# Two hardware loops over octets written out as straight code with constant semaphore counts

## What is computed

```python
x = x + tanh(g_xattn[0]) * L0_xattn(ctx, layernorm(x), mask)   # 2 heads of 64, rms-normed q and k
x = x + tanh(g_ffn[0])   * L0_ffn(layernorm(x))                # 16 experts x 64 slots, soft dispatch/combine
x = x + tanh(g_xattn[1]) * L1_xattn(ctx, layernorm(x))         # 8 heads of 128
x = x + tanh(g_ffn[1])   * L1_ffn(layernorm(x))                # 8 experts, top 2 of them by a router

# L0_ffn: logits = x . slots; dispatch = softmax over tokens; combine = softmax over slots
#   slots = dispatch^T x; eout = (gelu(slots Wg + bg) * (slots Wu + bu)) Wd + bd; out = combine eout
# L1_ffn: y_e = (silu(x Wg_e) * (x Wu_e)) Wd_e; out = sum_e share_e * y_e, share 0 but for the top 2
```

## Time and profile before

| | us |
|---|---|
| median of three executions | 1766.96 |
| the profiled execution | 1768.4 |
| its span (first to last instruction) | 1766.6 |
| TensorE busy with matmuls | 1585.7 (90%) |
| TensorE weight loads | 1320.4 (75%) |
| VectorE busy | 1113.1 (63%) |
| ScalarE busy | 965.1 (55%) |
| GpSimd busy | 396.7 (22%) |

### The profile page before, as it was taken

How to read it: one execution, slowest core, us unless ns; L and a number is a source line. 1 busy time by engine, 2 the same in 40 slices (tenths; PEclk the granted TensorE clock), 3 DMA queues, 4 the chain that set the end, 5 groups by cost and what they waited for, 6 DMA issues and landing times. The chain is left out here.

```text
span 1766.6 us, 35984 instructions
## 1 busy us (share of the span) xinstructions
PE 1585.7 (90%) x12837; PEld 1320.4 (75%) x12837; DVE 1113.1 (63%) x2407; ACT 965.1 (55%) x1470; POOL 396.7 (22%) x346
## 2 busy tenths in 40 slices
PE   1677479999999999999999998699989979999998
PEld 1566368888887888878888886577777747888887
DVE  6688476666666666666666654366666656555555
ACT  1678366676676666666666664366556543222222
POOL 2243332222322223222232221122223200000000
PEclk9899799999999999999999999799999989999999
DMA  8100000000000000000000000200000020000000
GB/s 224 34 1 0 16 1 2 1 2 1 2 2 3 1 1 2 2 3 1 2 2 1 2 1 25 74 1 1 0 0 0 1 73 1 7 12 6 6 6 12
DMA packets 31166, 23.43 MB, mean 13 GB/s; under 512 B 3161, under 2 KB 28721, under 8 KB 30898
## 3 DMA queue, kind: packets, MB, share of 16 engines
q1 hardware_dynamic: 31026, 21.56, 4.4%
HBM read 19.46 MB, written 2.10 MB: 12 GB/s over the span
## 5 line engine op out<-in xcount | busy, mean ns | idle before, releaser
L887 ACT ACTIVATE gelu<-psG,b_cols 128x512 f32<-128x512 f32 x256 | 176.1, 688 | 178.2 <-PE psG L137 164.4
L987 PE MATMUL psDown<-w_down,hidden 128*64 128x128 f32 x4096 | 252.0, 276 | 0.6 <-DVE expert_out L774 0.6
L768 DVE SCALAR_TENSOR_TENSOR hidden<-psU,b_cols,gelu 128x512 f32<-128x512 f32 x256 | 189.5, 747 | 88.5 <-ACT gelu L887 66.1
L987 PEld LDWEIGHTS psDown<-w_down,hidden 128*64 128x64 f32 x4096 | 220.9, 137 | 18.4 <-DVE expert_out L774 9.0
L1632 ACT ACTIVATE silu<-psG 128x512 f32<-128x512 f32 x128 | 76.4, 597 | 213.2 <-PE psG L137 207.6
L774 DVE TENSOR_TENSOR expert_out<-psDown,b_down 128x512 f32<-128x512 f32 x128 | 88.2, 689 | 157.5 <-PE psDown L987 147.2
L723 POOL TENSOR_TENSOR combine_sum<-combine_sum,combineT 128x512 f32<-128x512 f32 x48 | 61.2, 1276 | 350.9 <-ACT combineT L901 350.9
L1694 PEld LDWEIGHTS psY<-w_downT,hidden 128*128 128x128 f32 x1024 | 124.0, 191 | 5.8
L1694 PE MATMUL psY<-w_downT,hidden 128*128 128x128 f32 x1024 | 124.3, 275 | 0.0
L1586 DVE TENSOR_TENSOR hidden<-psU,silu 128x512 f32<-128x512 f32 x128 | 88.5, 692 | 54.6 <-PE psU L137 51.3
L1575 DVE SCALAR_TENSOR_TENSOR x<-psY,combine,x 128x128 f32 (+1 forms) x256 | 72.7, 345 | 78.1 <-PE psY L1694 77.8
(11 more groups left out here) (326 smaller groups left out, 3627.1 us busy)
## 6 DMA issues: line engine op xcount, KB each, us to landing
ctx<-in_ctx SPq DMA_DIRECT2D x8, 512.0 KB, 7.2
x<-in_x SPq DMA_DIRECT2D x4, 512.0 KB, 5.5
w_gate_raw<-in_L_ffn_Wg SPq DMA_DIRECT2D x1, 2048.0 KB, 12.8
w_up_raw<-in_L_ffn_Wu SPq DMA_DIRECT2D x1, 2048.0 KB, 18.3
out<-x SPq DMA_DIRECT2D x8, 256.0 KB, 2.3
w_kv<-in_L_xattn_Wkv SPq DMA_DIRECT2D x1, 1024.0 KB
w_down_raw<-in_L_ffn_w_down SPq DMA_DIRECT2D x1, 1024.0 KB, 10.4
kv<-in_L_ffn_slot_embeds SPq DMA_DIRECT2D x1, 512.0 KB, 4.2
```

Source lines behind the costliest of these rows:

```text
L768: dve.scalar_tensor_tensor(hid[e][:, half, :], U[half][:], bcol[:, 1, 4 * ch + 2 * e + half:][:, 0:1], gel[half][:], ALU.add, ALU.mult).th ...
L887: act.activation(gel[half][:], G[half][:], ACT.Gelu, bias=bcol[:, 0, 4 * ch + 2 * e + half:][:, 0:1]).then_inc(s["gelu"], 1)
L987: last = pe.matmul(DN[e * SEQ:(e + 1) * SEQ, j, :], hid[e][:, half, b * SEQ:(b + 1) * SEQ], wd[:, 2 * ch + e, half, :], start=(half == 0 a ...
```

## The change

Both hardware loops become Python loops, so that every octet is emitted once with constant counts and addresses. No instruction of the computation is added, removed or reordered; each engine's order of octets, chunks and slots stays.

```diff
@@ walk
     body(-1, 1)
     body(0, 0)
-    if OCTETS > 2:
-        with eng.Fori(0, (OCTETS - 2) // 2) as turn:
-            body(turn * 2 + 1, 1)
-            body(turn * 2 + 2, 0)
+    for o in range(1, OCTETS - 1):
+        body(o, o % 2)
     body(OCTETS - 1, 1)
@@ stage_experts1
         def octets(eng, body):
-            body(0)
-            with eng.Fori(1, OCTETS) as o:
+            for o in range(OCTETS):
                 body(o)
```

## The result

The changed kernel takes 1752.91 us (median of 4 executions, 1752.04 to 1754.48), the kernel before 1766.26 beside it (4 executions, 1765.21 to 1768.95): a ratio of 0.9923, 95% interval 0.9906 to 0.994. The forecast was 1753.9.

A forecast was written before the change was run, and what follows sets the result against it. It took TensorE to bound both experts stages, short waits through VectorE and ScalarE besides TensorE in attention 1, and VectorE to be mostly busy in attention 0. 8.6 + 4.0 + 0.3 + 0.2 = 13.1 off 1766.96 gave 1753.9 us, range 1750 to 1762.

The forecast's parts named there:

- The jumps, 6.1: Experts 0, two far jumps back: 4.78 us of TensorE idle time and 1.36 after it go; 6.1 us, bounds 4.8 and 6.1.
- The octet edges, 1.2: Experts 0, edges into octets 1 to 6: first gate product starts 0.20 us sooner after its copy; 1.2 us in all.
- Chunks 4 and 6, 1.0: Experts 0, looped octets: these chunks drop from 13.13 to the straight 13.05 us; 1.0 us over six octets.
- `finish`, 0.3: Experts 0, VectorE's register instructions elsewhere in an octet: 0.3 us, between 0 and 0.6, from 0.1 for each octet.
- Attention 1, 4.0: Six looped octets: transposes stop waiting for hats, 1.58 us, and earlier hats shorten a later idle time, 2.4; bounds 1.0 and 4.4.
- the second gain: Attention 1: hats beginning sooner shorten TensorE's 1.12 us idle before the output product to 0.7; 0.40 x 6 = 2.4 us.
- The rest: Attention 0 gains 0.3 us (bounds -0.5 and 1.5), experts 1 gains 0, the final store comes 0.2 sooner.
- (a): Rival: only the jumps count, register instructions elsewhere hide behind waits that stay; 6.1 of 13.1 remain, 1760.9 us; chance 0.12.
- (b): Rival: slower, as straight code must be fetched every octet, about 20 more blocks at 2.5 us each; 1804 us; chance 0.04.
- (c): Rival: no change that can be told, since waits reappear later in experts 0 and attention 1; within 3.5 us of 1767; chance 0.06.
- (d): Rival: the other ten jumps also held TensorE, unseen, at 2.39 us each; 24 us more gained, 1730 us; chance 0.02.

The follow-up runs named there:

- The stage alone: The kernel before with only experts 0 written as straight code, the other loops kept; 1757.61 us, ratio 0.9942.
- the stage run alone: The kernel before with only attention 0 and experts 1 written as straight code; 1769.17 us, ratio 1.0001.
- short body: The changed kernel with octets 1 to 6 of experts 1 looped again, two turns of three octets; 1754.19 us, one execution.
- late hats: The changed kernel with one idle VectorE tile added ahead of the normed tiles in each octet of attention 1; 1754.22 us, ratio 0.992.
- early hats: The changed kernel with attention 1's normed tiles made in slots 4 and 5 of the octet before; 1749.0 us, ratio 0.9891.
- all announced: The kernel before, loops kept, jumps back announced on all four engines in the three stages using `walk`; 1768.82 us, ratio 1.0006.
- long body: The changed kernel with experts 1 looped as two turns of three octets and its down product computed three times; 1983.68 us, one execution.
- TensorE announced: The kernel before, loops kept, jump back announced in experts 0 on TensorE alone; 1764.13 us, ratio 0.9979.
- with VectorE: The kernel before, loops kept, jump back announced in experts 0 on TensorE and VectorE; 1762.82 us, ratio 0.9972.

## Why the prediction was right, and which terms were off

The mechanism was the forecast one in every large part. That the medians came out within 0.3 us of the forecast gain of 13.1 is in part luck, since by the trace the parts add up to 14.9.

**The jumps, 6.1.** Right. Chunk 7 of octets 2 and 4 went from 17.04 and 17.37 to 14.70; with 0.20 of each counted at the edges, that is 4.6. Octet 5's first chunk gave 1.39 at full clock. Together 6.0. The 1.36 in the sum is octet 5's 108.95 over octet 1's 107.59; that a slower clock made it, rows 4 alone, with a mean of 0.89 over the chunk, leave to inference, and a narrower window of the kernel before shows it: 0.50 from 781.33 to 784.30 and 1.00 from 784.40 to the chunk's end.

**The octet edges, 1.2.** Right, measured 1.35: five gave 0.20 and the edge into octet 1, where the loop was entered, 0.35.

**Chunks 4 and 6, 1.0.** Right, 1.1: chunk 4 is 13.03 to 13.05 in every octet now.

**`finish`, 0.3.** Mis-sized, in the step that took "what one such row costs" once for each octet. Chunk 1 went from 13.58 to 13.69 down to 13.48 or 13.49: 0.1 and 0.2 us by turns, 0.9 in six octets. Experts 0 in all: its octets 0 to 6 last 759.65 before and 750.30 after, 9.35 against the 8.6 of the sum. The stage alone gave as much.

**Attention 1, 4.0.** The mechanism was right and the second gain too small: 1.57 and 6 x 0.58 = 3.5 instead of 1.58 and 2.4. The idle time before the output product came down to just the 0.7 forecast, and the transposes wait no more. What was mis-sized is the step that equated the gain with that idle time. Two rows of the kernel before stand beside rows 6 here, L1251 and L1254, with the transposes:

```profile
1174.54 0.69 DVE L1251 TENSOR_REDUCE neg_max<-psS 128x4 f32<-128x512 f32 x1
1174.73 0.63 PE L1412 MATMUL psX<-ident,ctx_hat 128*128 128x128 f32 x4
1175.36 0.69 DVE L1254 TENSOR_TENSOR probs<-psS,neg_max 128x512 f32<-128x512 f32 x1
```

Measured from the octet's first scores (1172.33 before, 1161.19 after), the output product starts 5.48 us later in rows 6 and 4.84 later now, 0.64 sooner. The hats start 0.42 sooner (0.12 behind the first scores before, 0.30 ahead of them after) and their tiles take 0.04 less, as forecast. Left out were the register instruction between L1251 and L1254, whose starts were 0.82 apart and are 0.72 apart now, and some 0.1 between the copy and the product. Of the 0.64, 0.58 reach the octet. TensorE's own share, seen in that the transposes start 2.40 behind the first scores before and 2.19 after, was there in octet 1 too: "in octet 1 TensorE goes straight on" overlooked a wait of 0.2.

**The rest.** Attention 0 was to give 0.3: octets 1 to 6 gave 1.2 together, but the clock took it back at the stage's end (37.7 to 38.1 us from octet 7 on instead of 36.8 to 37.0). The 0.3 of this pair of traces is within what the stage differs by from trace to trace, 193.2 to 194.5 us looped and 193.1 to 194.1 straight, and the median of the stage run alone gave nothing: the 0.3 came true by chance. Experts 1 gave 0. At the end, VectorE's last update ends at 1746.90 and the store follows at once, the 0.2 of the sum:

```profile
1745.77 1.13 DVE L1572 SCALAR_TENSOR_TENSOR x<-psY,combine,x 128x128 f32<-128x128 f32 x4 [0.66 <-PE psY L1691]
1746.92 0.37 SPq L1480 DMA_DIRECT2D out<-x  x1
```

The parts add up to 9.35 + 5.05 + 0.3 + 0.2 = 14.9, 1.8 over the sum. The profiled pair has 1.5 more: attention 1 up to the start of its octet 1 took 73.3 us before and 71.6 after. That isn't the change's. This piece takes 71.3 to 71.9 us in eight of the thirteen traces, looped and straight ones among them, and 73.4 to 73.8 in four (before, short body, late hats, early hats; 74.8 with all announced). In the longer form octet 0 lasts 32.6 to 32.8 instead of 31.6, with a stretch at a granted clock of 0.50 of 3.4 us inside it (at 1146.2 in the kernel before, at 1136.3 in the short body's), and some 0.9 more is lost ahead of it. How often an execution takes the longer form isn't known, so the medians may hold some of it too; they differ by 13.4, their interval reaching from 10.6 to 16.6.

**The rivals.** (a) Only the jumps count: out by attention 1 alone. (b) The stream must be fetched: 17 more blocks were fetched, near the 20 forecast, and no octet is longer than looped; experts 1 in straight code is not slower. That the loops bring no block after their first turn holds for attention 1 and experts 1 alone: in attention 0 the trace of before has one at 150.0. (c) No change: out. (d) All jumps cost: out, and with the body lengths now for a reason: ten of the twelve jumps close TensorE bodies of about 409 (attention 0), 469 and 958 instructions, under the 1,403 whose jump took 0.24 us, and took 0.21 to 0.24 themselves.

## What to carry to other kernels

Count the instructions of a loop's body for each engine apart, registers and weight loads too: as long as it is short (here up to 1,403 on TensorE and 216 on VectorE) the jump is free behind queued work (0.24 us, the octet at its 36.64), and past the limit (here at 2,939 and 384) each turn costs some 3 us on that engine (3.36 and 2.93), of which the kernel feels what isn't covered by slack (1.85 and nothing), and the clock may fall behind it (here to 0.50 for 3.4 us). Where a chain of short waits goes through several engines, look for register instructions ahead of its links, since what is lost there can reach the end nearly whole (0.58 of 0.64 us here); taking the work that starts the chain out of it (here, hats an octet earlier) gives more than making it quicker (0.65 us an octet on top of 0.58). A gain ahead of a thinly filled stretch may be lost to TensorE's clock there (here 1.2 us gained and 0.7 to 1.3 lost), so cost it at the end of the stage and not at its octets.

## What the runs showed of the hardware that was not expected

- A far jump held TensorE for 3.4 to 3.9 us, VectorE for 2.8 to 3.3 and ScalarE for 2.6 and 2.8, and GpSimd, with 135 instructions in its body, for 0.2. VectorE's limit is much lower than TensorE's: 384 instructions were too many for it, 1,403 not for TensorE.
- The granted clock fell to 0.50 for 3.4 us behind the second jump alone in two executions (at 780.9 and 781.4) and behind both in a third (563.3 and 781.7). The idle time alone doesn't settle it: it fell behind 2.80, 2.68, 2.62 and 2.35 us of it, and not behind 2.47 and 2.51 (first jump of the first two) nor 1.60 (long body) nor 0.48 (announced).
- An announced jump costs 0.37 us instead of 3.5 to 3.9 on TensorE, but leaving the loop then cost 0.8 (TensorE announced), 1.1 (with VectorE) and 1.8 us (all four) in the next chunk. With three turns nothing was won by announcing everywhere (ratio 1.0006), and 3.7 and 4.9 us by announcing in experts 0 alone (0.9979 and 0.9972), less than half of the straight stage's 10.
- A loop of one trip with known bounds had its index folded into constants (650 ALU_OP instructions at TensorE's waits became 14); a test of registers needs something else.
